# A two-layer decoder on one core: the second cross attention's values are computed one step later, and every engine's order of work is merged anew

## What is computed

```
x = LN(x + L0_attn(x))            # 16 heads of 16, rotary positions
x = LN(x + L0_xattn(x, ctx, ctx)) # 8 heads, decaying weights, causal
x = LN(x + L0_ffn(x))             # rounded activations, ternary weights
x = LN(x + L1_attn(x))            # 16 heads of 16
x = LN(x + L1_xattn(x, ctx, ctx)) # 16 heads: q from x; k and v from ctx
x = LN(x + L1_ffn(x))
```

## Time and profile before

| | |
|---|---|
| median of three runs | 1827.99 us |
| the profiled execution's own time | 1826.03 us |
| its span, first to last instruction | 1824.4 us |
| TensorE busy | 1566.8 us (86%) |
| VectorE busy | 1175.5 us (64%) |
| ScalarE busy | 966.2 us (53%) |
| mean granted TensorE clock | 0.957 |

### The profile page before, as it was taken

How to read it: one execution, slowest core, us unless ns; L and a number is a source line. 1 busy time by engine, 2 the same in 40 slices (tenths; PEclk the granted TensorE clock), 3 DMA queues, 4 the chain that set the end, 5 groups by cost and what they waited for, 6 DMA issues and landing times.

```text
span 1824.4 us, 31797 instructions
## 1 busy us (share of the span) xinstructions
PE 1566.8 (86%) x12546; PEld 1001.5 (55%) x12546; DVE 1175.5 (64%) x2087; ACT 966.2 (53%) x1717; POOL 228.0 (12%) x233
## 2 busy tenths in 40 slices
PE   6489878979997887889999798888899989788898
PEld 3246545546764554645666465455566546455467
DVE  4855697664475677676347678876445667886632
ACT  2077454565435755456534664655544566456662
POOL 5200110001111011000112001000012101100000
PEclk9589799999999998999999999999899999899999
DMA  7510023321211011422211101233122201123200
GB/s 229 171 57 2 1 77 95 93 68 36 93 53 47 1 42 41 122 62 73 59 58 58 48 1 42 70 102 94 33 64 67 73 19 32 51 72 100 74 2 23
DMA packets 115747, 114.34 MB, mean 63 GB/s; under 512 B 10515, under 2 KB 101395, under 8 KB 115603
## 3 DMA queue, kind: packets, MB, share of 16 engines
q1 hardware_dynamic: 115282, 111.28, 20.1%
q10 hardware_dynamic: 320, 1.05, 0.3%
HBM read 68.91 MB, written 42.99 MB: 61 GB/s over the span
## 4 chain that ended last, share of the span: by engine, by line
PE 37%; DVE 9%; ACT 6%; DMA 4%; issue 2%; SPq 1%; POOL 0%; DVEq 0%; ACTq 0%
PE psum L686 6%; PE psum L796 5%; PE psum L931 5%; PE psum L679 4%; PE psum L923 4%; ACT PB L998 3%; DVE nm L1169 3%; PE psum L759 2%; PE psum L778 2%; DMA QK<-heads_dram 2%; DMA heads_dram<-U 2%; PE psum L673 2%; PE psum L719 2%; PE psum L807 1%; PE psum L863 1%
## 5 line engine op out<-in xcount | busy, mean ns | idle before, releaser
L1169 DVE TENSOR_REDUCE nm<-psum 128x4 f16<-128x1024 f32 x384 | 456.1, 1223 | 120.0 <-PE psum L759 118.0
L998 ACT ACTIVATE PB<-psum 128x1024 f32<-128x1024 f32 x384 | 383.7, 1023 | 225.0 <-PE psum L796 117.2
L1344 POOL TENSOR_TENSOR XO<-XO,row_b 128x512 f32<-128x512 f32 x80 | 103.1, 1291 | 1170.0 <-ACT XT L969 1148.7
L796 PE MATMUL psum<-PB,V 128*32 128x256 f32 x3072 | 210.0, 393 | 10.9 <-ACT PB L998 7.3
L759 PE MATMUL psum<-QK 48*128 48x256 f16 x1536 | 148.3, 289 | 68.1 <-DVE nm L1169 18.9
L778 PE MATMUL psum<-QK 49*128 49x256 f16 x1536 | 145.8, 278 | 53.7 <-ACT PB L998 25.6
L759 PEld LDWEIGHTS psum<-QK 48*128 48x128 f16 x1536 | 55.6, 97 | 154.8 <-issue 64.4
L778 PEld LDWEIGHTS psum<-QK 49*128 49x128 f16 x1536 | 51.9, 95 | 152.7 <-issue 55.3
L796 PEld LDWEIGHTS psum<-PB,V 128*32 128x32 f32 x3072 | 84.5, 110 | 85.9 <-issue 33.4
L923 PE MATMUL psum<-XT,W 128*128 128x256 f32 x512 | 121.4, 387 | 0.2 <-ACT XT L969 0.2
L931 PE MATMUL psum<-W,PB 128*128 128x256 f32 x512 | 116.6, 383 | 0.1
(11 more groups left out here) (158 smaller groups left out, 2654.4 us busy)
## 6 DMA issues: line engine op xcount, KB each, us to landing
QK<-heads_dram SPq DMA_DIRECT2D x96, 512.0 KB, 3.7
heads_dram<-U SPq DMA_DIRECT2D x288, 128.0 KB, 2.0
XO<-in_x SPq DMA_DIRECT2D x16, 256.0 KB, 3.2
Y<-in_ctx SPq DMA_DIRECT2D x16, 256.0 KB, 3.3
out<-XO SPq DMA_DIRECT2D x16, 256.0 KB, 4.1
W<-in_w SPq DMA_DIRECT2D x2, 1024.0 KB, 6.2
QK<-GN SPq DMA_DIRECT2D x96, 4.0 KB
heads_dram<-QK ACTq DMA_DIRECT2D x4, 256.0 KB, 8.7
```

What stands on the lines that cost most here:

```text
L796: ins = pe.matmul(b[SLOT * j:SLOT * j + SLOT, at:at + TOK], value(L, t, PAIRS * e + u, HEADS, HD, SLOT), src, start=(t == 0), stop=(t == T ...
L998: act.activation(PB[L][:, unit % PBUF, :], b[:, 0:1024], ACT.Exp, scale=HD ** -0.5)\
L1169: dve.tensor_reduce(nm[L][:, :, :, unit].rearrange("p t e -> p e t"), b[:, 0:1024].rearrange("p (e t k) -> p e t k", e=2, t=TT), AX.X, ALU ...
L1344: pool.tensor_tensor(stream(L, it), stream(L, it), row_b[:, occ:occ + 1, :].to_broadcast([P, TT, DIM]), ALU.add).then_inc(xb_ready[L], 1)
```

## The change

It has two parts. In `lane_steps()`, the step `v 2` stands behind `proj 1` and ahead of that projection's norm, not in front of `oT 1`. And all five strings of `TURNS`, and `PLACES`, are replaced by others of the same length (1905, 1377, 1014, 192 and 294 steps, 1777 banks). No instruction, shape, buffer or semaphore is added or taken away.

```
         if a == 1:
             add("qk", 2, 1)
             add("stack", 2, 1)
-            add("v", 2)
         add("oT", a)
         if a == 2:
             add("loadx", 0, 0, 1)
         add("proj", a)
+        if a == 1:
+            add("v", 2)
         add("norm", NORM_OF[a])
...
 TURNS = {
     "pe": (
-        "0001123200211322430301232100103003200022201222212111113132033313330000310020202200220322020320332330"
...
+        "0003311002231122200134322110000300302201120222211112121331323033033000103020222002022032022033023303"
...
     "sp": (
-        "0011223340002022421311331043424134000033330222211113020003123320322131121001300030202033331321222322"
...
+        "0011223340002021211321444330321434000303332022211113002003312303221231121001003000322033331312222321"
```

More of the change, by code:

```diff
@@ L166 @@
[L166 to L175, removed]
@@ L196 @@
-    "dve": (
[L197 to L207, removed]
+        "0003311002231122200134322110000300302201120222211112121331323033033000103020222002022032022033023303"
@@ new lines @@
+        "1310232210321101221110112213003023332033003110310303212202023200300320231301310320023010110203101032"
+        "2120121332132322303323231313113012312123322322203120123002302012012211012112311133201323031300130110"
+        "0321132223001010202023203321033131213311321132213220320120031222101312111321110121210212313211212122"
+        "31133"),
+    "act": (
+        "0001313232142002211330212000003100202220002202322032033302333023331011301021121311001322130323012223"
+        "0031331211232233301021031131032020013110023030312232031220313231233011211201001210001110000003030303"
+        "3300233303330322322232223322212321213110122110101121210001100301100313102333032230322003300013020023"
+        "0021120113022223103211133333311123312202333220022100000122000021021201103101101130103033300132331333"
+        "0320003200322123022230132212111023311102111331220120301233322122011302300131110232211113323332233023"
+        "1332121200200021000000120112122130012313003331313130333032332233222322321222221102111122110112101200"
+        "0311000110001313033032333023300200300022130023110221112030223231332113112331332102023023322221000012"
+        "2000000121202111101300113310003323100333133303200032001223230222322320123131112011102331112122301233"
+        "3002122101032103301121130221311133233221331120333210220120002102001002012012100213100313103330333333"
+        "2323232223322222323022210022110011121112111111030001133133310002303333022022000000301322200211223110"
+        "2123111031120332133123323302203231203200022100200001202100111311003110003133331332001333023000320222"
+        "0322013232212303213111021101333211121202133322001221010312012313110221311103332332233123023112021032"
+        "0002010201200020110201310021101331333033323333223322223322122323211221110111221120101200013100311301"
+        "00010033233332333203221203222010012223001113211111131212212313212112211033213"),
@@ new lines @@
+    "3423207102460460264204603346020604365022604027026024062410462414206520426106214027426052704260421424"
+    "0724602464042716462570261262046044270402624705241264036204063430604641464260641206241224265264267462"
+    "2624315266404125641646252415620451604265246120742607307126403207030406202052046204624107620424025106"
+    "5063402724061234062043066402670240420560460250600620546046406244027245240246432036063044205125610462"
+    "4127460425516025616262042640230640452472042270524621326220464021642602643106462462643214302512726042"
@@ L236 @@
+    "05204650460460364004640624612562412043602764042063401252067617030712621520376"
 )
```

91 lines of the change are left out of this document (43 added, 48 removed).

## The result

In runs on one chip the kernel after took 1816.6 us (median of 6, 1808.41 to 1829.31), the kernel before 1832.24 us (median of 6, 1827.45 to 1837.24): ratio on record 0.9927, 95% interval 0.99 to 0.9954 (the quotient of the two medians is 0.9915). The first three of these runs of before took 1827.45 to 1830.03 us, the other three 1834.46 to 1837.24, so part of this gain is the scatter of before. So the change makes the kernel some 0.5 to 0.7% faster, 9 to 13 us; I had forecast 4.7 us. The sign was right, most of the working was not, and that the forecast came near is in good part luck. Three runs of before, of 1849.43, 1850.6 and 1851.88 us, belong to a slower state of the chip and are left out everywhere.

The account below looks back on a forecast made before the run. No engine was full, TensorE led at 86% busy, with handoffs between engines of about 1 us; moved step -4.2, start -2.5, end +2, other merges 0 gave -4.7 us: 1823.3 us on the median, range 1812 to 1837.

Parts of the forecast that it names:

- The moved step, -4.2: Values step moved from before `oT 1` to behind `proj 1`: 27.7 us moves from 8% to 24% idle, -4.2 us.
- filled anyway: Rival: moved step finds no more idle time than it leaves, start's holes turn up elsewhere; 1828 us, no change; chance 0.18.
- from 21.6 us towards 10: Sign of being right: TensorE's idle time between `proj 1` and `xT 3` falls this far.
- Own chains: Rival: lanes bound by their own chain, four passes save 9.7 us, with the start 12.2: 1815.8 us; chance 0.12.
- the 0.685 us that I had allowed: VectorE's addition before the norm: norm up to 0.685 us late if the root is ready first, 2.7 us over four passes.
- The start, -2.5: First pass: two waits from SyncE's queue close, -2.5 and -1.8 us, against +1.8 for later ropes; -2.5 us, bounds -5 and +3.
- my bound of +3: Start's upper bound: lane 3's second stack, behind `qk 1` and two more DMAs, opens a hole as large as the closed one.
- 94 to 97: Sign of being right: the us at which the last `max` of the first pass ends.
- +1.8: Start: lane 3's `ctx` and `xT` run later, so VectorE's ropes come 1.3 to 2 us late; +1.8 us.
- The end, +2: Last pass: attention steps pulled ahead of lane 0's `up1` leave TensorE idle around 1730 to 1760; +2 us, bounds 0 and +8.
- The other merges, 0: Elsewhere orders differ by swaps of neighbours in both directions, no row giving a sign; 0, bounds -8 and +8 us.
- the rivals I had written of the clock: Another order moves pauses and clock dips; four more dips of 2 us, 1831 us; chance 0.11, shared with unfavourable swaps.

Follow-up runs that it names:

- after_again: The changed kernel itself, no edit, timed in a second batch against the kernel before: ratio 0.9953 (0.9934 to 0.9973).
- move_alone: Orders of the kernel before, with only the sixteen values steps put directly behind their lane's projection: ratio 1.0134 to the kernel before.
- end_of_before: Orders and banks of the changed kernel to about 1690 us, then those of the kernel before: ratio 1.0024 to the kernel before.
- first_620: Orders and banks of the changed kernel up to about 620 us, then those of the kernel before: ratio 0.9994 to the kernel before.
- first_250: Orders and banks of the changed kernel for the first 250 us, then those of before; no values step moved: ratio 1.003 to the kernel before.

## Why the prediction was right or wrong

**The moved step, -4.2: wrong, and it is the step of the working that failed.** "At equal total work the gain is the difference of how idle the two places are" treats the idle share as a chance that moved work falls into a hole. Idle in the two places together was 33.4 us before, 32.4 after and 31.7 in after_again: 1.0 to 1.7 us, not 4.2, though all merges were made for the new list. This is what my rival 'filled anyway' said of the step. The reader should read idle time there as TensorE waiting for a step of another engine, which extra work does not fill but delays: 0.4 of 27.7 us was filled in move_alone (idle 21.2 for 21.6). The fall "from 21.6 us towards 10" that would have shown me right did not come.

**Own chains: no.** The lane's time from `heads 1` to `max 2`, mean of 16, was 32.7 us before and 33.2 after. `oT 1` does come 2.7 us sooner behind the heads, but the norm ends 1.3 us later behind the root, twice the 0.685 us that I had allowed, and `xT 3` starts 0.6 us later behind the norm.

**A trap here.** The lane's time from `exp 2` to `heads 2` falls from 43.2 to 39.7 us, which looks like the gain. The sums of these 16 stretches, before and after:

```profile
sum 691.30, PE 629.69 PEld 400.19 DVE 337.58 ACT 378.09 POOL 82.53; mean PE 39.36 PEld 25.01 DVE 21.10 ACT 23.63 POOL 5.16
```
```profile
sum 634.80, PE 574.42 PEld 362.79 DVE 321.69 ACT 367.90 POOL 81.26; mean PE 35.90 PEld 22.67 DVE 20.11 ACT 22.99 POOL 5.08
```

Idle time is 61.6 and 60.4 us: in these stretches TensorE is busy 55 us less, with work of other lanes that is done elsewhere. A lane's phase that got shorter is no time won until the idle time or the clock says so.

**The start, -2.5: wrong in sign.** The first 104 steps take 2.6 us more (4.7 in after_again; the ranges of the two orders overlap, their means are 128.1 and 130.5). The queue did what I worked out up to one point. SyncE's queue, TensorE and VectorE after:

```profile
62.10 2.64 SPq L644 DMA_DIRECT2D QK<-heads_dram  x2
...
68.79 10.55 SPq L576 DMA_DIRECT2D W_o<-in_w_proj  x16
...
81.68 0.54 SPq L638 DMA_DIRECT2D heads_dram<-U  x1
82.28 1.41 SPq L649 DMA_DIRECT2D QK<-GN  x2
86.77 0.34 SPq L644 DMA_DIRECT2D QK<-heads_dram  x1
```
```profile
67.40 2.12 PE L760 MATMUL psum<-QK 48*128 48x256 f16 x16 [3.75 <-DMA QK<-heads_dram]
...
90.25 1.04 PE L760 MATMUL psum<-QK 48*128 48x256 f16 x8 [4.00 <-DMA QK<-heads_dram]
```
```profile
69.55 18.29 DVE L1170 TENSOR_REDUCE nm<-psum 128x4 f16<-128x1024 f32 x16 [0.28 <-PE psum L760]
90.89 9.25 DVE L1170 TENSOR_REDUCE nm<-psum 128x4 f16<-128x1024 f32 x8 [3.05 <-PE psum L760]
```

Lane 1's stack goes at 62, as forecast, and 16 weights take 10.55 us (10.8 forecast). But lane 3's second stack, forecast for 82, goes at 86.77: it must follow its own keys' writes, issued until 82.22, and I counted the queue's issues and not that wait. It opens a hole of 4.00 us where the one of 4.03 closed: the condition of my bound of +3, which I had named and not taken. The other wait, 4.70 us before, is 3.75 us after, though VectorE stood only 0.28 us behind it. The first `max` starts at 57.24, not 54.18, the last ends at 100.14, not 98.38 and not at 94 to 97: the row of `max` steps itself is 1.3 us shorter, and the 3.1 us by which it starts late, for which I had +1.8, outweigh that.

**The end, +2: right.** The last stretch took 111.6 us before, 113.6 and 115.1 after, and end_of_before gets it back. In the last 124 us, measured from the end as the earlier trace rows are:

```profile
1682.30:1722.30 40.00, 31.57 (x331) 18.28 (x331) 29.16 (x40) 22.44 (x34) 0.00 (x0) 1.00 0.21 64
1722.30:1802.30 80.00, 78.65 (x495) 62.41 (x492) 19.02 (x56) 35.11 (x70) 6.23 (x5) 1.00 0.03 11
```

TensorE is idle 9.8 us where it was 7.6, the whole of it ahead of 1722 and not in the last 80 us as I had placed it.

**The other merges, 0: the term that was missing.** Stretches 2, 3 and 5 give -8.2, -2.3 and -11.2 us, stretch 4 +2.7, 6 and 7 together -3.3; my bound was 8 either way. Stretches 4 to 7 hold the moved steps too, so not all of it is this term's. Part of that trace's -17.7 us is the luck of its clock. How much can be read from the stretches at the lower clock level: their sums in before, after and the second trace of after:

```profile
sum 157.95, PE 126.63 PEld 68.75 DVE 121.27 ACT 46.50 POOL 24.00; mean PE 5.51 PEld 2.99 DVE 5.27 ACT 2.02 POOL 1.04
```
```profile
sum 137.24, PE 103.34 PEld 54.38 DVE 115.17 ACT 44.09 POOL 18.26; mean PE 4.92 PEld 2.59 DVE 5.48 ACT 2.10 POOL 0.87
```
```profile
sum 174.53, PE 134.26 PEld 73.41 DVE 132.62 ACT 48.56 POOL 15.40; mean PE 4.97 PEld 2.72 DVE 4.91 ACT 1.80 POOL 0.57
```

At half the clock, half of TensorE's busy time there is the price, an estimate: 63.3, 51.7 and 67.1 us. The rest of the busy time is then 1503.5, 1500.8 and 1500.4 us, nearly the same in all three, which bears the estimate out. Without that price the spans are 1761.1, 1755.0 and 1752.5 us. So of the 17.7 us some 11.6 are clock and 6 are not; the second trace pays 3.8 us more for its clock than before does and is still 4.8 us shorter. A gain of 6 to 9 us that is not the clock's agrees with the 8.7 at a common clock. Of it 3 to 5 us is less idle time of TensorE, lower in both traces in stretches 2, 3, 5 and 6 and higher in 1, 4 and 8; which steps brought that is open.

Among the rivals I had written of the clock: "Another order moves the pauses, and with them the dips. Four more of them". They moved, but the sum did not change: over the 18 runs of after and the 72 of before whose clock is on record the mean is 0.953 for both. Stretch 2 is a dip less that shows beyond the scatter. Stretch 5 takes 374.0 to 381.2 us in the four traces of the unmodified list with the new order beyond 620 us and 384.1 to 387.2 in before, first_620 and first_250; I isolated no single pause there.

**In sum.** The steps that failed are the moved step, which gave 1.0 to 1.7 us of idle time where I had 4.2, and the start, which cost 2.6 us and more where I had a gain of 2.5. The two terms that made the forecast's sign did not come, the end came as forecast, and the term that I had put at 0 must have been the largest, since the whole came out at -9. Sign and nearness of the 4.7 us are luck.

## What to carry to other kernels

An order that is written out over several in-order engines prices a step by its place in the list and not by its duration: taking 24 us out gave nothing measurable, and moving 28 us cost 22 to 55 us until all orders were merged again. This was seen in one kernel with these two sets of orders. So don't fill holes by arithmetic on idle shares; ask which engine's step TensorE waits for in the hole. And give a new merge a term of both signs for the clock: look in the old trace for places at 0.5 to 0.6 and ask whether the new order still has the pauses ahead of them. Then compare the kernels at equal mean clock, since a dip that goes in one place can come back in another.

## What the runs showed of the hardware that I had not expected

- The mean granted clock differs from run to run of one kernel (0.946 to 0.962 in the six of after), and the time follows it: 1829.31 and 1808.41 us at these two.
- Pauses of 0.35 and 0.59 us within 3 us were followed by about 15 us at 0.50 to 0.62, 6.6 us lost. The stretch had a clock of 0.90 to 0.95 in all six traces of this order; in another order of the same steps it was 1.00, in eight traces of eight.
- With 24 us of TensorE's work less its mean clock was lower: 0.953 to 0.944 and 0.953 to 0.945, twelve runs each.
- TensorE's busy time less half of what fell at the lower level is 1503.5, 1500.8 and 1500.4 us in three traces whose busy time is 1566.8, 1552.5 and 1567.5: at the lower level it does half the work.
